# One-hot matrix on ScalarE, the last products before a sum, and one flag matmul in a graph message kernel

## What is computed

```
w_m = (efeat @ W_msg + b_msg).reshape(E, 16, 16)
w_a = (efeat @ W_attn + b_attn).reshape(E, 16, 16)
h_src = feat[src][:, :, None]
e1 = w_m * h_src
e2 = w_a * h_src
ex = exp(e2 - segment_max(e2, dst)[dst])
attn = ex / segment_sum(ex, dst)[dst]
ft = segment_sum(e1 * attn, dst).sum(axis=1)
x = layernorm(x + ft)
```

## Time and profile before

| | |
|---|---|
| median of 3 runs | 1730.8 us (1730.54 to 1731.0) |
| profiled execution, its own time | 1732.84 us |
| its span | 1731.0 us |
| mean granted TensorE clock | 0.962 of full |
| VectorE busy | 1537.4 us, 89% |
| TensorE busy | 1354.0 us, 78% |
| GpSimd busy | 974.1 us, 56% |
| ScalarE busy | 889.1 us, 51% |

### The profile page before, as it was taken

One profiled execution on the slowest core, in us unless ns is written; L12 is line 12 of the kernel. 1 busy time (PEld: TensorE's weight loads), 2 busy tenths in 40 slices (PEclk: granted clock), 3 DMA queues, 4 the chain that ended last, 5 costly groups with the idle time before them and its releaser, 6 DMA issues. The chain is left out here.

```text
span 1731.0 us, 20720 instructions
## 1 busy us (share of the span) xinstructions
PE 1354.0 (78%) x5767; PEld 690.3 (40%) x5767; DVE 1537.4 (89%) x1614; ACT 889.1 (51%) x1842; POOL 974.1 (56%) x878
## 2 busy tenths in 40 slices
PE   0002899999999999999999999999999999998400
PEld 0001444444444444444444444444444444444200
DVE  8534899999999999999999999999999999998458
ACT  1002566666666666666666666666665555554100
POOL 5777777777676676776777676676661000000170
PEclk9999899999999999999999999999999999999655
DMA  4314344444444444444444444444443222221150
GB/s 109 76 19 112 93 122 117 125 122 117 126 119 116 127 119 117 127 118 116 128 118 117 127 118 117 127 118 118 126 116 105 94 81 80 95 71 54 56 147 18
DMA packets 174990, 182.94 MB, mean 106 GB/s; under 512 B 47056, under 2 KB 130328, under 8 KB 174878
## 3 DMA queue, kind: packets, MB, share of 16 engines
q1 hardware_dynamic: 140958, 158.74, 29.1%
q0 software_dynamic: 33920, 22.89, 8.3%
HBM read 92.36 MB, written 89.41 MB: 105 GB/s over the span
## 5 line engine op out<-in xcount | busy, mean ns | idle before, releaser
L488 POOL DMA_INDIRECT split<-x_parts,edge_src x784 | 880.6, 1123 | 351.3 <-issue 220.1
L781 PE MATMUL bank_sum<-em,row_onehot 128*128 128x512 f32 x1760 | 891.4, 609 | 31.3 <-ACT sum_rows L647 31.0
L1024 DVE TENSOR_TENSOR em<-bank_prod,h_rows 128x1024 f32<-128x1024 f32 x440 | 524.2, 1212 | 64.1 <-PE bank_prod L769 58.1
L781 PEld LDWEIGHTS bank_sum<-em,row_onehot 128*128 128x128 f32 x1760 | 299.0, 189 | 222.8 <-issue 184.1
L1042 DVE TENSOR_TENSOR em<-em 128x1024 f32<-128x1024 f32 x220 | 267.7, 1217 | 3.5 <-ACT em L606 3.5
L769 PE MATMUL bank_prod<-w_rows,partsT 100*128 100x512 bf16 x880 | 269.3, 388 | 1.0 <-DMA partsT<-tile_table 0.6
L647 ACT COPY sum_rows<-bank_sum 128x512 f32<-128x512 f32 x220 | 126.8, 576 | 275.6 <-PE bank_sum L781 254.6
L1067 DVE TENSOR_TENSOR em<-em,bank_max 128x2048 f32<-128x2048 f32 x110 | 250.7, 2279 | 3.2 <-ACT node_max L638 3.2
L606 ACT ACTIVATE em<-em 128x2048 f32<-128x2048 f32 x110 | 210.5, 1914 | 3.6 <-DVE em L1067 3.6
L630 ACT COPY chunk_fwd<-bank_max 128x512 f32<-128x512 f32 x110 | 64.5, 586 | 276.7 <-PE bank_max L712 276.7
L769 PEld LDWEIGHTS bank_prod<-w_rows,partsT 100*128 100x128 bf16 x880 | 86.7, 99 | 249.2 <-issue 203.1
(11 more groups left out here) (165 smaller groups left out, 1171.0 us busy)
## 6 DMA issues: line engine op xcount, KB each, us to landing
sums<-sum_rows SPq DMA_DIRECT2D x110, 512.0 KB
rec<-split_records SPq DMA_DIRECT2D x220, 144.0 KB, 2.2
split_records<-split SPq DMA_DIRECT2D x97, 288.0 KB, 2.1
mask<-tile_table SPq DMA_DIRECT2D x110, 192.0 KB, 3.2
split<-x_parts,edge_src POOLq DMA_INDIRECT x784
rel<-tile_table SPq DMA_DIRECT2D x110, 64.0 KB, 3.0
edge_feat<-in_features SPq DMA_DIRECT2D x97, 64.0 KB
flag<-tile_table SPq DMA_DIRECT2D x110, 2.0 KB
```

The source lines that it names most:

```text
L488: return nc.gpsimd.indirect_dma_start(out, None, src, bass.IndirectOffsetOnAxis(idx, 0))
L781: mm = nc.tensor.matmul(bank_sum[:, :], row_onehot[:, t % RING, g, :], em[:, t % RING, s * GROUPS + g, :, :, :].rearrange("p i m o -> p (i ...
L1024: V.tensor_tensor(em[:, v, 2 * j:2 * j + 2, :, :, :].rearrange("p s i m o -> p s i (m o)"), bank_prod[j % 2][:, :, :].rearrange("p s (i x) ...
```

## The change

Three edits:

1. `sel` is made by ScalarE, in two instructions: the absolute value of `rel` minus the partition's number into a new tile `off_sel`, then relu of one minus that, which is 1 where they are equal and 0 elsewhere. They stand behind `end_places` in ScalarE's loop, ahead of `part2`; VectorE's comparison is gone.
2. `give_features` has one flag matmul with 8 rows of weights and 128 columns for both groups, first in the accumulation, and then the six products. The tile `flag8` has a row for each slot and group, and the constant `big8` fits it; the flags' load has 8 rows of 256 bytes instead of 4 of 512.
3. In TensorE's loop `products(t + 1, 3)` stands ahead of `sum_slots(t - 2, 0, [1])` instead of behind it.

```
-                sp.dma_start(flag4[:, w, :], tab_d[t:t + 1, 4 * WIDE:8 * WIDE].rearrange("t (s c) -> (t s) c", s=SLOTS)
+                sp.dma_start(flag8[:, w, :], tab_d[t:t + 1, 4 * WIDE:8 * WIDE].rearrange("t (k c) -> (t k) c", k=SIDE)
...
+            def select(t):
+
+                if not tile(t):
+                    return
+                w = t % 2
+                act.wait_ge(rel_landed[w], rounds(t, 2))
+                nc.scalar.activation(off_sel[:, :], rel[:, w, :], ACT.Abs, bias=minus_part[:, 0:1]).then_inc(sel_off, 1)
+                act.wait_ge(sel_off, t + 1)
+                since(act, h_ready, t - 1)
+                nc.scalar.activation(sel[:, w, :], off_sel[:, :], ACT.Relu, bias=one_col[:, 0:1],
+                                     scale=-1.0).then_inc(sel_ready, 1)
...
                 end_places(t + 1)
+                select(t + 3)
                 part2(q - 1)
...
+                nc.tensor.matmul(bank_t[0][:, 0:GROUPS * SLOTS * FEAT], flag8[:, w, :], big8[:, :],
+                                 start=True, stop=False)
                 for g in range(GROUPS):
                     rows = bank_t[0][:, g * SLOTS * FEAT:(g + 1) * SLOTS * FEAT]
                     parts = rec_h16[:, v, g, :].rearrange("p (s d k) -> p s d k", s=SLOTS, d=3)
                     for d in range(3):
-                        nc.tensor.matmul(rows, sel[:, w, g * P:(g + 1) * P], parts[:, :, d, :],
-                                         start=(d == 0), stop=False)
-                    mm = nc.tensor.matmul(rows, flag4[:, w, g * P:(g + 1) * P], big4[:, :], start=False, stop=True)
+                        mm = nc.tensor.matmul(rows, sel[:, w, g * P:(g + 1) * P], parts[:, :, d, :],
+                                              start=False, stop=(g == GROUPS - 1 and d == 2))
                 mm.then_inc(h_ready, 1)
...
                 give_features(t + 2)
+                products(t + 1, 3)
                 sum_slots(t - 2, 0, [1])
-                products(t + 1, 3)
...
-            def select(t):
-
-                if not tile(t):
-                    return
-                w = t % 2
-                v_eng.wait_ge(rel_landed[w], rounds(t, 2))
-                since(v_eng, h_ready, t - 1)
-                V.tensor_scalar(sel[:, w, :], rel[:, w, :], part_iota[:, 0:1], None, ALU.is_equal).then_inc(sel_ready, 1)
```

More of the change, by code:

```diff
@@ L97, in gnn_kernel @@
         zeros = sb("zeros", [P, COLUMNS * WIDE])
-        slot_iota = sb("slot_iota", [P, SLOTS, FEAT])
-        big4 = sb("big4", [SLOTS, SLOTS * FEAT], BF16)
+        slot_iota = sb("slot_iota", [P, GROUPS, SLOTS, FEAT])
+        big8 = sb("big8", [SIDE, GROUPS * SLOTS * FEAT], BF16)
         minus_part = sb("minus_part", [P, 1])
@@ L167, in gnn_kernel @@
         sel = sb("sel", [P, 2, WIDE], BF16)
-        flag4 = sb("flag4", [SLOTS, 2, WIDE], BF16)
+        flag8 = sb("flag8", [SIDE, 2, P], BF16)
+        off_sel = sb("off_sel", [P, WIDE], BF16)
         h_rows = sb("h_rows", [P, 2, GROUPS, SLOTS * FEAT])
@@ L264, in gnn_kernel @@
         flags_landed = [sem(f"flags_landed{u}") for u in range(2)]
+        sel_off = sem("sel_off")
         sel_ready = sem("sel_ready")
@@ L484, in _ @@
             iota(place_iota[:, :, :], [[0, GROUPS], [1, P]], 0)
-            iota(slot_iota[:, :, :], [[1, SLOTS], [0, FEAT]], 0)
+            iota(slot_iota[:, :, :, :], [[1, GROUPS], [GROUPS, SLOTS], [0, FEAT]], 0)
             def gather(out, src, idx):
@@ L860, in _ @@
             v_eng.wait_ge(iotas, 6)
-            link(V.tensor_scalar(big4[:, :], slot_iota[0:SLOTS, :, :].rearrange("p s k -> p (s k)"), part_iota[0:SLOTS, 0:1],
+            link(V.tensor_scalar(big8[:, :], slot_iota[0:SIDE, :, :, :].rearrange("p g s k -> p (g s k)"), part_iota[0:SIDE, 0:1],
                                  BIG, ALU.is_equal, ALU.mult))
@@ L1080, in _ @@
                 shift(t)
-                select(t + 3)
                 rest1(q)
```

## The result

The changed kernel takes 1687.8 us (median of 4 runs, 1687.0 to 1689.2) against 1730.9 us before (4 runs): a ratio of 0.9752, interval 0.9735 to 0.9769, 43 us or 2.5% faster. The prediction said 1690 us, 1684 to 1707. The profiled execution has a span of 1687.1 us.

A forecast was written before the change was run, and what follows sets the result against it. A TensorE-ScalarE ring, not VectorE, was taken as the bound; its stretch shrinks from 2.04 to 1.66 us, 0.38 saved over 105 tiles is 39.9 us, plus about 1 for the ramp: 1730.8 to 1690 us, range 1684 to 1707.

The forecast's parts named there:

- The late tiles' argument: After 1336.8 us VectorE loses 0.4 us a tile, yet the tile still takes 12.97 us, so VectorE isn't the limit.
- the ring: TensorE and ScalarE waiting for each other: 2.92 us through ScalarE plus TensorE's stretch from 706.92 on set the tile.
- Step 1: TensorE's features: one flag matmul first, then six products; one weight change instead of four, each 0.12 to 0.13 us.
- The term for the new flag matmul: TensorE, from the flag matmul's start to the next product: 0.13 plus 0.03 for the added columns, 0.16 us.
- Step 2: TensorE's swap: products ahead of the sum, 0.06 us to start and 0.43, then the sum at 0.86.
- the ramp: About five first tiles before the steady period; VectorE's removed instruction and flag changes there give about 1 us, an estimate.
- Step 3: Matrix moved to ScalarE: VectorE loses 0.20 us, ScalarE gains 0.96 us inside its 2.33 us hole; nothing counts.
- VectorE as the limit: Rival: VectorE, 89% busy, bounds the kernel; the full 0.65 us a tile would be saved, 1662 us; 4%.
- The swap that gives back: Rival: products pay the sum's full surcharge or a new wait opens; 0.20 us a tile saved, 1709 us; 16%.
- The gap that isn't the rows: Rival: the 0.13 us between TensorE's matmuls come from something else; no visible change, 1729 to 1732 us; 4%.
- The slower rival: ScalarE's added 0.96 us delay SyncE's flag load; at a 4.0 us landing +0.19 us a tile, 1751 us; 5%.
- The room: From SyncE's last flag issue at 703.49 to TensorE's use at 706.92: 3.4 us, against a landing of 1.6 us.

The follow-up runs named there:

- u3_sel_only: The kernel before with only the 0/1 matrix `sel` made by ScalarE instead of VectorE: 1730.0 us, ratio 0.9997.
- d4_four_more: The changed kernel with four more ScalarE instructions like the one making `off_sel`, into a spare tile nobody reads: 1763.2 us, ratio 1.0188.
- c1_casts_first: The changed kernel with ScalarE's two casts of partsT ahead of the exponent: 1651.4 us, ratio 0.9541.
- u1_flags_only: The kernel before with only the one flag matmul (`flag8`, `big8`), no swap, the matrix on VectorE: 1694.9 us, ratio 0.9796.
- p2_pad_after: The changed kernel with the flags' weights and their constant padded with zeros from 8 to 128 rows: 1676.0 us, ratio 0.968.
- u4_no_sel: The changed kernel with the 0/1 matrix back on VectorE: 1686.6 us.
- c2_casts_first_no_sel: The changed kernel with ScalarE's casts of partsT ahead of the exponent and the 0/1 matrix back on VectorE: 1704.0 us, ratio 0.9838.
- d2_two_more: The changed kernel with two more ScalarE instructions like the one making `off_sel`, into a spare tile nobody reads: 1691.5 us, ratio 0.9789.
- c5_seven_gathers: c2_casts_first_no_sel with seven gathers of source features a preparation step instead of eight, leaving out part of the work: 1659.4 us, ratio 0.9586.

## Why the prediction was right

**What bounds the kernel.** Right. The late tiles' argument (0.4 us less of VectorE's work, the same 12.97 us) is borne out from both sides: u3_sel_only takes 0.20 us from VectorE and gains nothing; d4_four_more overfills ScalarE's hole, and c1_casts_first takes the ring's wait away, and both move the steady early tile by what the ring says.

**Step 1** was right in kind, and measured 0.32 us a tile with the sum behind it (u1_flags_only). The gap of 0.12 to 0.13 us at a change between weights of few and many rows was read from one tile's starts, with nothing to tell the rows from the rest; p2_pad_after shows that it is the rows. The term for the new flag matmul, 0.16, measured 0.16.

**Step 2**: 0.06 us was taken for the start of the products behind the six, between 0.03 and 0.24; the record shows 0.03, the lower bound (the sixth product starts five steps of 0.03 after 715.34, the products at 715.52). With it the saving is 0.41 instead of 0.38: 105 x 0.41 = 43 us, as measured. That is the term that was mis-sized, by 3 us. The swap alone is worth 0.09. The 1 us that the sum adds for the ramp is not shown: the ramp's three tiles take 43.0 us before, 41.0 after, and 40.5 in both u3_sel_only and u4_no_sel, so its spread is larger than the term.

**Step 3**: nothing, as forecast, and all of it hidden: 0.93 us of ScalarE (709.35 to 710.28; forecast 0.96) in a hole of 2.33. The rule of the Trainium skill, page ScalarE: Activation LUTs, section Rules for kernel authors, that relu belongs on VectorE, holds for the prices, and not for the kernel as it stands. In c1_casts_first, where VectorE is the limit, the move does count, 0.19 us a tile (12.25 against 12.44 in c2_casts_first_no_sel), and it is VectorE that must be spared: there the rule points the wrong way.

**The rivals.** VectorE as the limit, and with it the rule of the Trainium skill, page Perfetto Trace Analysis, section Identifying the Most-Contended Engine, to help the engine of highest occupancy first: not so, 1662 us didn't come; VectorE at 90% was 0.3 us a tile from its limit. The swap that gives back: no, the products start 0.03 us behind the sixth product. The gap that isn't the rows: no, by p2_pad_after. The slower rival, flags that come late because something ahead of them in SyncE's queue waits: it happened once in 300 to 1300 us of the changed kernel, two more instructions on ScalarE bring six such waits, and GpSimd without slack brings 24. The one, in the changed kernel:

```profile
573.21 0.29 SPq L426 DMA_DIRECT2D partsT<-tile_table  x1
```

```profile
576.98 0.21 PE L766 MATMUL bank_t<-big,flag 8*128 8x128 bf16 x1 [0.99 <-DMA partsT<-tile_table]
```

From issue to use it is 3.8 us, 0.3 us more than the wait for the cast would have been. The room was reckoned as 3.4 us, and that was right; the landing was taken as 1.6 us from a single row of the ramp, and this one took over twice that. So the change leaves no margin against the slowest landings, and d2_two_more, which takes another 1.0 us of room, shows it.

VectorE's idle time ahead of the first times_features was forecast at 0.3 us. The bracket says 0.18 to 0.23, since a record ends 0.08 us later than the next could start; by the starts it is 0.3, and c1_casts_first shows VectorE's own round bare, 12.25 us (12.33 was forecast, by the bracket's 0.45 for a hole that is 0.5 by the starts).

## What to carry to other kernels

Where engines wait for each other in a ring, find a stretch of the same run in which one engine has less to do: if the period doesn't change, that engine isn't the limit, whatever its busy share. Then read the starts of small matmuls one by one: a gap that comes at each change of the weights' row count goes away with fewer changes, or with zero rows. An edit's worth is that of the moment: the padding was worth 12 us before the casts were moved and nothing in the median after, the matrix's move nothing before and 0.19 us a tile after.

The best version here is c1_casts_first, 1651.4 us, 4.6% under the kernel before.

## What the runs showed of the hardware

- A matmul of 64 or 128 columns with weights of 4 or 8 rows delays the next with weights of 128 rows to 0.13 or 0.16 us after its start; with 128 rows, zeros among them, it is 0.03 or 0.07. In the other direction it is the same: 0.13 from a product with 128 rows to a flag matmul with 4, and 0.10 us beyond the 0.43 of a product with 100 rows when a flag matmul with 8 follows (c1_casts_first). Weights of 100 rows behind weights of 128 showed no such gap (0.03).
- An fp32 sum behind bf16 matmuls of 64 columns takes 0.94 us instead of 0.86, and bf16 products there 0.44 instead of 0.43.
- A GpSimd gather, 0.94 us alone, that starts while VectorE runs four operations back to back that read and write SBUF only, mostly ends 0.9 us after VectorE's next operation begins, and takes up to 2.0 us. Some are passed over until the first operation that reads PSUM, up to 4.35 us: none of 147 in the kernel before, 48 of 105 in c2_casts_first_no_sel, one in nearly every tile of c5_seven_gathers. What decides between the two was not found.
- The two small flag rows, issued by SyncE, were in use 1.6 us after the issue in the ramp, and not before 3.8 us in one steady tile of the changed kernel.
